# State-space stage: its loop over the four sequences written out, and the first sequence's step sizes moved ahead of most of the first gate pair

## What is computed

```python
zxbcdt = u @ in_proj_w.T
z, xBC = zxbcdt[..., :D_INNER], zxbcdt[..., D_INNER:D_INNER + CONV_DIM]
dt = softplus(zxbcdt[..., D_INNER + CONV_DIM:] + dt_bias)      # step sizes, 16 heads
xBC = silu(conv_b + sum(conv_w[:, k] * xp[:, k:k + l, :] for k in range(4)))
dA_cs = cumsum(dt * A)                                         # -> decays between tokens
y = (Y_diag + Y_off) + x * D_skip                              # from x*dt, B, C and the decays
y = rmsnorm(y * silu(z)) @ out_proj_w.T
```

## Time and profile before

| | us |
|---|---|
| median of 3 runs | 2509.34 |
| lowest and highest run | 2494.38, 2510.12 |
| the profiled execution | 2489.68 |
| its span (first to last instruction) | 2487.9 |
| mean granted TensorE clock in it, share of full speed | 0.97 |

### The profile page before, as it was taken

One profiled execution on the slowest core, in us unless ns is written; L12 is line 12 of the kernel. 1 busy time (PEld: TensorE's weight loads), 2 busy tenths in 40 slices (PEclk: granted clock), 3 DMA queues, 4 the chain that ended last, 5 costly groups with the idle time before them and its releaser, 6 DMA issues.

```text
span 2487.9 us, 32830 instructions
## 1 busy us (share of the span) xinstructions
PE 2216.5 (89%) x10235; PEld 1628.5 (65%) x10235; DVE 1873.4 (75%) x2846; ACT 1003.4 (40%) x2059; POOL 684.0 (27%) x544
## 2 busy tenths in 40 slices
PE   0689989979988899889879999999999998999998
PEld 0344444444445578677657788878888887888886
DVE  8989898998878865676666667768777786666665
ACT  3244343342352454454444444444434444322222
POOL 5434435335341544435431012121212210000000
PEclk9899999999999999999979999999999999999999
DMA  5001001001015432353341010010010101000001
GB/s 213 18 26 43 34 17 43 25 17 51 17 52 186 177 133 82 132 183 132 109 163 35 0 34 26 9 43 17 17 39 21 51 17 64 13 25 25 25 13 68
DMA packets 52811, 148.80 MB, mean 60 GB/s; under 512 B 5009, under 2 KB 5009, under 8 KB 48337
## 3 DMA queue, kind: packets, MB, share of 16 engines
q1 hardware_dynamic: 34144, 96.08, 10.8%
q10 hardware_dynamic: 12864, 32.81, 3.6%
q0 software_dynamic: 5680, 18.62, 2.5%
HBM read 113.14 MB, written 34.34 MB: 59 GB/s over the span
## 4 chain that ended last, share of the span: by engine, by line
issue 34%; PE 32%; POOL 12%; DVE 8%; POOLq 8%; ACT 2%; DMA 1%; ACTq 0%; DVEq 0%; SPq 0%
PE bank L341 9%; PE bank L343 9%; PE bank L342 9%; POOLq L496 2%; PE bank L2381 2%; POOL g_v L504 2%; POOL g_v L497 2%; POOLq L519 1%; POOLq L522 1%; POOL g_s L518 1%; POOLq L769 1%; POOLq L508 1%; POOL g_v L520 1%; POOL g_s L510 1%; POOL g_eu L503 1%
## 5 line engine op out<-in xcount | busy, mean ns | idle before, releaser
L2256 PE MATMUL bank<-um,w_in 128*128 128x512 f32 x576 | 264.8, 614 | 4.7 <-DVE lm L1577 4.6
L2256 PEld LDWEIGHTS bank<-um,w_in 128*128 128x128 f32 x576 | 110.6, 197 | 136.5 <-issue 129.2
L1182 ACT ACTIVATE probs<-bank,nmx 128x128 f32<-128x128 f32 (+3 forms) x256 | 131.8, 528 | 95.4 <-DVE nmx L2006 95.4
L341 PE MATMUL bank<-u_hi,aw_hi 128*128 (+1 forms) x384 | 157.2, 409 | 3.7 <-DVE u_lo L2043 3.7
L1190 ACT ACTIVATE pt_hi<-bank 128x512 fp32r<-128x512 f32 (+1 forms) x192 | 93.9, 526 | 154.6 <-PE bank L2381 154.6
L343 PE MATMUL bank<-u_hi,aw_lo 128*128 (+1 forms) x384 | 151.0, 393 | 0.0
L342 PE MATMUL bank<-u_lo,aw_hi 128*128 (+1 forms) x384 | 150.8, 393 | 0.0
L2432 PE MATMUL bank<-mw,bu_hi 128*128 (+1 forms) x312 | 128.1, 411 | 15.2 <-DVE mw L1861 7.3
L451 DVE TENSOR_TENSOR_SCAN g_s<-decay,g_s 128x512 f32<-128x512 f32 x96 | 133.6, 1432 | 8.0 <-POOL g_v L497 8.0
L341 PE MATMUL bank<-u_hi,fw_hi 128*128 128x512 f32 x352 | 136.9, 389 | 0.0
L342 PE MATMUL bank<-u_lo,fw_hi 128*128 128x512 f32 x352 | 136.9, 389 | 0.0
(11 more groups left out here) (385 smaller groups left out, 6202.2 us busy)
## 6 DMA issues: line engine op xcount, KB each, us to landing
m_stage<-in_moe SPq DMA_DIRECT2D x21, 1024.0 KB, 6.7
y_slot<-m_o ACTq DMA_DIRECT2D x39, 256.0 KB, 2.0
g_v<-in_fT SPq DMA_DIRECT2D x18, 512.0 KB, 3.6
gates<-g_v SPq DMA_DIRECT2D x18, 512.0 KB, 2.8
f_stage<-in_ffn SPq DMA_DIRECT2D x11, 768.0 KB, 4.2
u_g<-gates SPq DMA_DIRECT2D x8, 1024.0 KB, 8.4
aw_in<-in_att SPq DMA_DIRECT2D x4, 1280.0 KB, 5.8
w_in<-in_w_in ACTq DMA_DIRECT2D x1, 4640.0 KB, 16.2
```

Source lines behind the costliest of these rows:

```text
L341: nc.tensor.matmul(out, hi_w, hi_x, start=start, stop=False)
L1182: A(probs[:, h % 2, PR_AT[qb]:PR_AT[qb] + w], S_[bk][:, c0:c0 + w], ACT.Exp, bias=nmx[:, h % 2, qb:qb + 1], scale=SCALE, accum_out=rsum[:, ...
L2256: mm = M(dst[:], w_in[:, k, c0:c0 + P], um[:, k, :], start=(k == 0), stop=(k == KC - 1))
```

## The change

The loops over b become Python loops on ACT, DVE and PE, so that the four trips stand one after the other in each stream, with constants for counts and addresses, and the `If` blocks on b become plain ones. POOL's and SP's loops stay. For b = 0 alone the order changes, on DVE:

- ahead of the step sizes stays only `scans((0, 0), 0)`; `scans((0, 0), 1)` and `dens((0, 0))` stand behind them, ahead of `taps(0)`; `inverse((0, 0))` stands behind `taps(0)` and w2
- `clamp(first, 0)` and `clamp(first, 1)` stand behind `taps(1)`, `scans(first, 0)` behind `taps(2)`, `scans(first, 1)` behind `taps(3)` and csT, ahead of `dens(first)`

and on ACT: `gate(first, 0)` behind the three steps of the sums, and `gate(first, 1)` behind the first two z chunks' silu. Here `first` is `mamba_pair(0, 0)`, the second gate pair of all.

```diff
@@ ACT
-            with act.Fori(0, BATCH) as b:
+            for b in range(BATCH):
                 act.wait_ge(dt_proj, b + 1)
                 A(dtT, EB[0:HEADS_M, :], ACT.Copy).then_inc(dt_copied, 1)
-                gate(mamba_pair(b, 0), 0)
+                if b:
+                    gate(mamba_pair(b, 0), 0)
                 act.wait_ge(dt_abs, b + 1)
                 A(d_e[:], d_a[:], ACT.Exp, scale=-1.0).then_inc(dt_exp, 1)
-                gate(mamba_pair(b, 0), 1)
+                if b:
+                    gate(mamba_pair(b, 0), 1)
...
                         A(csT[0:HEADS_M, :], EB[0:HEADS_M, :], ACT.Copy).then_inc(ct_hi, 1)
+                        if b == 0:
+                            gate(mamba_pair(b, 0), 0)
...
                         z_silu(0)
                         z_silu(1)
+                        if b == 0:
+                            gate(mamba_pair(b, 0), 1)
@@ DVE
             mamba_input(0)
             scans((0, 0), 0)
-            scans((0, 0), 1)
-            dens((0, 0))
-            inverse((0, 0))
-            with dve.Fori(0, BATCH) as b:
-                step.base = b * DVE_MAMBA
-
-                clamp(mamba_pair(b, 0), 0)
+            for b in range(BATCH):
+                step.base, step.n = b * DVE_MAMBA, 0
+
+                if b:
+                    clamp(mamba_pair(b, 0), 0)
                 dve.wait_ge(dt_raw, b + 1)
...
                                 ALU.mult).then_inc(dA_ready, 1)
-                clamp(mamba_pair(b, 0), 1)
+                if b:
+                    clamp(mamba_pair(b, 0), 1)
+                else:
+                    scans((0, 0), 1)
+                    dens((0, 0))
...
                         V.tensor_tensor(w2[:], SM[:, 128:128 + NB], csn[:], ALU.add).then_inc(cs_neg, 1)
+                        if b == 0:
+                            inverse((0, 0))
+                    elif b == 0 and q == 1:
+                        clamp(first, 0)
+                        clamp(first, 1)
+                    elif b == 0 and q == 2:
+                        scans(first, 0)
                     elif q < 3:
                         scans(first, q - 1)
...
                         step.wait()
+                        if b == 0:
+                            scans(first, 1)
                         dens(first)
...
-                with dve.If(b < BATCH - 1):
+                if b < BATCH - 1:
                     scans(fourth, 0)
                     scans(fourth, 1)
@@ PE
-            with pe.Fori(0, BATCH) as b:
+            for b in range(BATCH):
                 pe.wait_ge(u_ready, FIRST + b + 1)
```

More of the change, by code:

```diff
@@ L962, in _ @@
                 square(PAIRS - 1)
-                with act.If(b == BATCH - 1):
+                if b == BATCH - 1:
                     act.wait_ge(x_added, KC * (BATCH - 1))
@@ L968, in _ @@
                 A(rms_inv, SM[:], ACT.Sqrt, scale=1.0 / D_IN, bias=eps_c[:]).then_inc(rms_done, 1)
-                with act.If(b < BATCH - 1):
+                if b < BATCH - 1:
                     tanh_x(b + 1, (b + 1) % BATCH, txm, b + 1)
@@ L1700, in _ @@
                         clamp(fourth, 1)
-                with dve.If(b < BATCH - 1):
+                if b < BATCH - 1:
                     scans(fourth, 0)
                     scans(fourth, 1)
-                with dve.If(b == BATCH - 1):
+                if b == BATCH - 1:
                     for m in range(BATCH - 1):
```

## The result

| | before | after |
|---|---|---|
| median, us (8 runs each) | 2494.35 | 2479.15 |
| lowest and highest | 2488.17, 2510.12 | 2477.09, 2481.15 |
| the profiled execution, and its span | 2489.68, 2487.9 | 2477.09, 2475.4 |
| ratio, 95% interval | | 0.9932 (0.9906 to 0.9957) |

A forecast was written before the change was run, and what follows sets the result against it. DVE's total work was taken to bound the first sequence, and its three loop turns the later ones. Turns 6.2, reorder 2.5 and constants 1 sum to 9.7, so 10 off the median of 2509.3 gives 2499; range 2481 to 2510.

The forecast's parts named there:

- taking 10 from the median: Last step of the sum: 10 us gain taken from the shown runs' median of 2509.3, giving 2499.
- whole stage speeds up: Rival, chance 0.1: constants in place of registers take gaps out of every handover, 6 us more; 2493.
- Turns: DVE's three idles at L442, where its loop turns to the next sequence, vanish when written out: 6.2 us.
- slower: Rival, chance 0.07: longer straight code makes DVE pause for instructions, 2.2 us each; 2518, 8 us slower.
- Constants: Constant counts and addresses remove small gaps between DVE instructions: 1 us over all four sequences, bounds 0 and 6.
- The reorder: DVE's new order in the first sequence lets PE start chunk q=6 earlier: 2.5 us, range 0 to 4.6.
- q=6 at 129 or later: Sign on PE in the first sequence that the reorder gives nothing; the forecast had 126.9 instead of 129.5.
- loops alone: Rival, chance 0.2: the first sequence gives nothing, through POOL stretching DVE's scans or ACT's queue delaying first taps; 2503.
- The three new idles: New DVE waits in the reordered first sequence: for dt_raw 5.1, ahead of the second clamp 2, for POOL's add 2.4.
- hide under the wait for POOL: At ACT's gate(first, 1) in the first sequence, the first added table load of 1.28 was to cost nothing.
- three more stretches of 1 us: First sequence: if POOL stretches three more DVE scans or clamps by 1 us, nothing of the 2.5 is left.
- DVE sets the pace up to csT: First sequence: DVE is the limit until csT, so any gain from PE's clock in q=2 and q=3 stays hidden.

The follow-up runs named there:

- e3: The kernel before with only PE's and ACT's loops written out, DVE's loop kept; 2497.35 us, ratio 1.0014.
- e5: The kernel before with six filler matmuls in PE's pause ahead of the state sums; 2489.35 us, ratio 0.9968.
- e4: The kernel before with only the first sequence written out, in the new order, and loops over the other three; 2491.26 us, ratio 0.9973.
- e2: The kernel before with only DVE's loop written out, in the old order; 2483.22 us, ratio 0.9945.
- e1: The changed kernel with the first sequence back in its old order, all three loops written out; 2478.4 us, ratio 0.9915 to before.
- e11: The kernel before with a DVE memset of 2 tiles ahead of the loop; 2494.55 us.
- e12: The kernel before with a DVE memset of 4 tiles ahead of the loop; 2496.3 us.
- e8: The changed kernel with scans((0, 0), 1) moved back ahead of the step sizes, into DVE's pause; 2476.05 us, ratio 0.991.

## Why the prediction was right or wrong

**The base: this alone put the time out of the range.** I took 10 from the median of three runs, 2509.34. Later runs put the kernel before at 2494.35. Two of the three that I had, 2509.34 and 2510.12, belong to the upper group of its runs, which has 19 of 86. The step that failed is "taking 10 from the median": the profile on which the whole sum rests ran 2489.7, the lowest run 2494.4, and 2494.35 - 9.7 would have said 2484.7, with 2479.15 well inside. The rivals, which all start from 2509, share the mistake. Against 2494.35, the measured 15.2 is nearer to the 16 of *whole stage speeds up* than to my 10. Kernels with DVE's loop have such runs (before, 4 of 10 in e3, 1 of 10 in e5), and those with DVE's stream straight have none in 66. Why stays open.

**Turns, 6.2 predicted, 3.2 measured.** The mechanism was right: no issue idle after, at none of the three places, and e4 loses exactly the one turn that is no jump. The Trainium skill, "Runtime: NRT & Kernel Launch", section "Instruction fetch mechanics", has straight code prefetched and a taken branch to code outside the pages at hand stall. The traces agree, with 2.0 to 2.2 us per jump of DVE in the kernel before and no such pause in 680 us of straight code. These rows also settle the rival *slower*. The size was off: I took all of the idle as path, "DVE being 2.1 earlier is PE being 2.1 earlier", and did not look at what else would move. L442 slid under POOL's work and took 1.48 in place of 0.59, the operation of L1558 (L1554 before) 0.82 in place of 0.23. About 1.0 of 2.2 arrives, 1.1 by e4 and e5.

**Constants, 1 predicted, 3.1 measured** (0.9 in each of three later sequences, by e4's one; 0.4 in the last four residual additions, which take 4.71 us where they took 5.14). I called the gaps unpriced, but they could be read in the rows of before: L456 starts 0.14 behind its predecessor's end inside the loop (107.52), and 0.03 behind for pair (0, 0), which stands ahead of the loop with constants (71.39, behind the scans of 69.03). The rival *whole stage speeds up* had this mechanism with more than twice the size.

**The clock at the state sums, 0 predicted, 4.2 measured** (three waits of 1.6, priced by e5 at 1.6, 1.4 and 1.2). The row of 4.8 stood in the same list of waits as the earlier trace rows, and I passed over it. No instruction of it is touched by the change; the time depends on it all the same. That a looped trip meets it and a straight one mostly doesn't is what the runs show. The cause isn't.

**The reorder, 2.5 predicted, 0 measured.** The chain of steps was right in kind, and it came out 2.4 us late at its end, until nothing was left. "q=6 at 129 or later" was the sign that I had named for *loops alone*. Times are starts where nothing else is said:

| | predicted | after | why |
|---|---|---|---|
| dt_raw read | 79.0 | 79.88 | PE's dt projection 6.21 us, 5.25 before |
| PE's sums end | 91.5 | 91.7 | |
| taps(0) | 92.4 | 92.95 | |
| inverse ends | 98.4 | 98.9 | |
| clamp(first, 1) | 103.8 | 105.87 | ACT's table load of 1.28, the inverse 0.5 late |
| taps(2) | 104.7 | 107.68 | L443 at 1.49, not 0.42 |
| csT ends | 116.4 | 118.7 | scans(first, 0) 5.4, 5.9 counted |
| taps(4) | 124.6 | 126.90 | |
| q=6 | 126.9 | 129.26 | |

The three new idles are there (6.12, 2.69 and 2.38, predicted 5.1, 2 and 2.4) and so is the fourth that was kept. The largest slip is ACT's. Its timeline after:

```profile
97.67 1.28 ACT L908 ACT_TABLE_LOAD   x1
...
103.30 1.28 ACT L436 ACT_TABLE_LOAD   x1 [2.73 <-POOL g_v L520]
```

I had the load "hide under the wait for POOL". It stands behind the wait: 2.73 idle, then 1.28 of load, then the exponential. In the kernel before, such a load did lie under a wait; writing out ACT's loop moved it. At the third pair's gate in the second sequence, ACT before and, in the last row, after:

```profile
330.25 1.28 ACT L436 ACT_TABLE_LOAD   x1
332.52 0.63 ACT L436 ACTIVATE g_s<-g_v 128x512 f32<-128x512 f32 x1 [0.98 <-DVE g_s L479]
...
330.46 1.28 ACT L436 ACT_TABLE_LOAD   x1 [2.33 <-DVE g_s L479]
```

Before, the load comes first and the wait for DVE is what is left behind it; after, the wait comes first. At this gate e2, which keeps ACT's loop, is like before in all four sequences, and e1 and e3, which don't, are like after. In the later sequences it cost nothing that shows: e1's and e2's are all 166.9 to 167.1.

The rule weighed there (the Trainium skill, "ScalarE: Activation LUTs", section "Table sets: the hidden batching unit", group by table set) would have spoken against gate(first, 1) between two silus, and here it holds, at 1.28 a load and not 2.7.

The second slip is POOL beside the clamps. I had named three more stretches of 1 us as the point at which nothing is left. L443 was stretched by 1.07 twice, but the first time (101.70) that fell into the idle behind it; the second (106.27) was paid. The scans behind it took 0.5 less than I had counted. *Loops alone* was right about the first sequence, and close in its mechanisms: ACT's queue delayed the clamp, not the first taps, and POOL stretched the clamp, not the scans.

That "DVE sets the pace up to csT" did not hold for q=4 either: its chunk took 9.71 in place of 7.03, at a mean granted clock of 0.53 in 108 to 115, after PE had waited 3.69 for ACT's chunk, and PE came to csT at 119.59, when it was 0.9 old. The lower clock stayed hidden all the same, because taps(4) was later still (PE waits 1.10 at 129.26). Two small slips bear on nothing: *loops alone* is 2502 by its own terms, and 9.7 is eaten by the fifth pause of 2.2, not the fourth.

**The sum.** Predicted 6.2 + 1 + 2.5 = 9.7 in the stage; measured 3.2 + 3.1 + 0 + 4.2 = 10.5 of 12.2. The other 1.7 is not split: 0.7 lies in the later sequences, 0.3 at and in the first, 0.7 on DVE ahead of the last residual additions. The total came out near because two terms were too high by 5.5 and two too low by 6.3. That the sum is near 10 is luck, and only single parts undone could show it. The profiles differ by another 0.3 behind the stage and the medians by 3.0 more than the 12.2, in code that is the same. There, single profiles of all these kernels differ by up to 11 us (1726.9 to 1737.9 from the stage's end to the last instruction), so it is left open.

## What to carry to other kernels

Before an idle is counted as gain, move the instructions behind it by that much and see beside whose work they land; here about half of each turn was given back at once. Price the small gaps ahead of instructions with register addresses by comparing them with the same instruction where its address is a constant, and go through every row of the list of waits in the stage, also those that the change doesn't touch. Take the base from the run whose trace you argue with, above all when three runs span 16 us. And when a loop is written out, look where the table loads stand afterwards: ACT's moved from ahead of a wait to behind it.

## What the runs showed of the hardware

- DVE's jump back costs 1.9 to 2.3 us of idle (17 jumps in before, e3, e4, e5, e11 and e12), that of PE or ACT nothing that shows (e3). Without a jump, e4's first turn has none.
- On DVE the edge (L456) and the residual addition (L1723, after L1740), which wait for their predecessors, start 0.14 us behind them with registers for addresses and counts, and 0.03 with constants. Not every instruction with registers shows it: L464 starts 0.03 behind in both kernels.
- A table load on ACT takes 1.28 us. At the third pair's gate it lay ahead of the wait, and so hidden under it, with ACT's loop (before, e2), and behind the wait with ACT written out (after, e1, e3).
- A 128x512 tensor-scalar on DVE took 0.42 alone and 1.49 beside POOL's work (L443), and in the turn L442 went from 0.59 to 1.48.
- A pause on PE of 2.20 to 2.41 us was followed by a clock of 1.2 GHz in some sequences and 2.4 in others, and its length didn't decide (2.41 and 2.4 GHz in e4's second sequence, 2.21 and 1.2 GHz in e8's). Six short matmuls in it, 1.46 us in all, held 2.4 in all three later sequences of e5.
